# A two-layer graph network on one core: the first step's order, the last pair's tiles on three engines, and x in two transfers

## The reference

```python
# layer 0
h = jnp.maximum(_layernorm(x, axis=-1), 0.0)
query, keyt, value = h @ Wq.T + bq, h @ Wk.T + bk, h @ Wv.T + bv
weight = adj * jnp.exp(jnp.einsum('bqd,bkd->bqk', query, keyt))
weight = weight / jnp.sum(weight, axis=2, keepdims=True)
x = x + jnp.einsum('bqk,bkd->bqd', weight, value)
# layer 1
h = jnp.maximum(_layernorm(x, axis=-1), 0.0)
agg = jnp.einsum('bij,bjf->bif', adj, h) / jnp.maximum(deg, 1e-6)     # deg = sum of adj over its last axis
x = x + jax.nn.relu(jnp.concatenate([h, agg], axis=2) @ W.T)
```

## Time and profile before

| | |
|---|---|
| median of 3 runs | 1888.66 us (1887.45 to 1889.35) |
| the profiled execution's own time | 1885.8 us |
| its span | 1884.0 us |
| TensorE busy | 1866.5 us, 99% |
| VectorE, ScalarE, GpSimd busy | 1508.2, 894.1, 991.3 us |
| DMA | 370.70 MB, 197 GB/s over the span |

### The profile page before, as it was taken

The page is one execution under the profiler, slowest core; times in us unless marked ns, Lnnn a source line. Parts: engine busy times, 40 slices in busy tenths (PEclk is TensorE's granted clock), DMA queues, the critical chain, the costliest instruction groups (busy, mean ns, idle before and its releaser), DMA issues.

```text
span 1884.0 us, 29380 instructions
## 1 busy us (share of the span) xinstructions
PE 1866.5 (99%) x8900; PEld 1567.3 (83%) x8900; DVE 1508.2 (80%) x2677; ACT 894.1 (47%) x1661; POOL 991.3 (53%) x1032
## 2 busy tenths in 40 slices
PE   8999999999999999999999999999999999999998
PEld 5888888888888888888888888888888888888886
DVE  7788787887787888888877878887888778888776
ACT  4444544455444445444545444454445454444543
POOL 4655465464564554654644645545546546456452
PEclk9999999999999999999999999999999999999999
DMA  5766656656656656566666576565666665666632
GB/s 184 231 213 193 200 194 207 209 190 198 211 184 217 206 189 202 197 206 207 190 200 209 181 222 200 189 206 196 210 200 198 195 209 185 215 201 190 206 128 101
DMA packets 199809, 370.70 MB, mean 197 GB/s; under 512 B 18928, under 2 KB 116208, under 8 KB 199536
## 3 DMA queue, kind: packets, MB, share of 16 engines
q1 hardware_dynamic: 199792, 370.49, 61.4%
HBM read 266.60 MB, written 103.81 MB: 197 GB/s over the span
## 4 chain that ended last, share of the span: by engine, by line
PE 92%; DVE 3%; DMA 2%; POOL 1%; issue 1%; ACT 1%; SPq 0%; POOLq 0%; DVEq 0%
PE bank L532 30%; PE bank L533 30%; PE bank L534 30%; DMA turned_store<-blocks 1%; PE bank L550 1%; DVE h L1150 1%; POOL xb L417 0%; POOL hT_l L426 0%; DMA turned<-turned_store 0%; SPq L271 0%; DVE bank L1251 0%; DVE stats L1118 0%; POOL rs L405 0%; DVE x L1263 0%; DMA xb<-wk 0%
## 5 line engine op out<-in xcount | busy, mean ns | idle before, releaser
L421 POOL TENSOR_TENSOR hT_l<-turned,hT_h 128x512 fp32r<-128x512 f32 x122 | 155.3, 1298 | 348.4 <-ACT hT_h L852 348.3
L248 POOL TENSOR_TENSOR w_l<-w,w_h 128x512 fp32r<-128x512 f32 x64 | 83.5, 1304 | 377.4 <-ACT w_h L883 377.4
L1100 DVE STREAM_TRANSPOSE blocks<-h 128x512 f32<-128x512 f32 x252 | 163.7, 687 | 114.5 <-DMA turned_store<-blocks 113.8
L846 ACT ACTIVATE h<-x,rs 128x512 f32<-128x512 f32 x124 | 94.0, 806 | 236.9 <-POOL rs L411 236.9
L532 PE MATMUL bank<-hT_h,n_h 128*128 128x512 f32 x512 | 199.4, 389 | 1.2 <-DVE hT_l L1191 1.2
L532 PE MATMUL bank<-wv_h,hT_h 128*128 128x512 f32 x512 | 199.6, 390 | 0.0
L533 PE MATMUL bank<-wv_l,hT_h 128*128 128x512 f32 x512 | 199.6, 390 | 0.0
L533 PE MATMUL bank<-hT_l,n_h 128*128 128x512 f32 x512 | 199.2, 389 | 0.0
L534 PE MATMUL bank<-hT_h,n_l 128*128 128x512 f32 x512 | 199.2, 389 | 0.0
L534 PE MATMUL bank<-wv_h,hT_l 128*128 128x512 f32 x512 | 199.2, 389 | 0.0
L417 POOL TENSOR_TENSOR xb<-x_in,bv_b 128x512 f32<-128x512 f32 x128 | 167.6, 1322 | 8.9 <-issue 8.9
(11 more groups left out here) (154 smaller groups left out, 5307.9 us busy)
## 6 DMA issues: line engine op xcount, KB each, us to landing
turned_store<-blocks SPq DMA_DIRECT2D x126, 512.0 KB, 3.8
turned<-turned_store SPq DMA_DIRECT2D x504, 128.0 KB, 2.9
x_in<-x SPq DMA_DIRECT2D x32, 1024.0 KB, 5.8
n_h<-t_store SPq DMA_DIRECT2D x62, 512.0 KB, 4.5
n_l<-t_store SPq DMA_DIRECT2D x62, 512.0 KB, 5.7
out<-x SPq DMA_DIRECT2D x124, 256.0 KB, 2.1
n_h<-n_store SPq DMA_DIRECT2D x60, 512.0 KB, 4.6
n_l<-n_store SPq DMA_DIRECT2D x60, 512.0 KB, 5.7
```

What stands on the lines that cost most here:

```text
L248: engine.tensor_tensor(w_l[:, g], w[:, g], w_h[:, g].bitcast(F32), ALU.subtract).then_inc(w_split, 1)
L421: pool.tensor_tensor(by_blocks(hT_l, t), turned_tile(t), by_blocks(hT_h, t).bitcast(F32), ALU.subtract).then_inc(hT_split, 1)
L846: nc.scalar.activation(h[:, t, :], src[:, t, :], ACT.Relu, bias=rs[n][:, 1, t:t + 1], scale=rs[n][:, 0, t:t + 1]).then_inc(h_done[n], 1)
L1100: nc.vector.transpose(blocks[:, :, :, t % NT, :].rearrange("p j c b -> p c j b"), h[:, t, :].rearrange("p (c j b) -> p c j b", c=DT, b=Q)) ...
```

## The change

It has these parts.

- **SP.** x of pair 0 is loaded in two halves, one graph each, behind the first and the second rows of `wq` and `wk`. In `first_step` the two stores of `n` come first, T1's store moves behind both loads of turned blocks, next to T2's. The last pair's stores of tiles 0 and 1 wait for GpSimd's adds.
- **T2** is split into `kz_h` and `kz_l` (free by then) instead of `at_h` and `at_l`; its low part goes from GpSimd to VectorE.
- **GpSimd** in `first_step`: T1's low part moves behind the splitting of the weights, and the first two `low_hT` ahead of the fourth `mix`. In `final_step` it adds x for tiles 0 and 1.
- **ScalarE** in `first_step`: the exponentials come right behind `relu_norm`, ahead of `high_v` and T1; the copies of `hT` are put among those of `v`. In `final_step` it rectifies tiles 0 and 1 into `h`.
- **VectorE** in `first_step`: each `kz_l` follows its key bias, the statistics come behind them, `weigh(0, 0)` and `weigh(0, 1)` move to both sides of `turn_h(1, 1)`, the results and statistics of layer 0 come ahead of the last two key biases, and B11's low part moves to step 1, behind `kz_l`. In `final_step` it leaves L1255 out for tiles 0 and 1.

```diff
@@ SP, ahead of the steps
-                if o == 0:
-                    load_x(0)
+                if o < G:
+                    sp.dma_start(x_in[:, NT * o:NT * (o + 1), :], x_d[0][:, NT * o:NT * (o + 1), :]).then_inc(x_first[o], 16)
@@ SP, first_step
+                sp.wait_ge(n_split, DT)
+                sp.dma_start(n_d[0], n_h[:, :, :].bitcast(F32)).then_inc(n_stored, 16)
+                sp.dma_start(n_d[1], n_l[:, :, :].bitcast(F32)).then_inc(n_stored, 16)
                 store_blocks(0, 0, h_turned, NT, h_stored)
-                store_t(0, T1)
                 sp.wait_ge(h_stored[0], 16)
                 load_turned(0, 0, h_moved)
                 store_blocks(0, 1, h_turned, T, h_stored)
                 sp.wait_ge(h_stored[1], 16)
                 load_turned(0, 1, h_moved)
-                store_t(1, T2)
+                store_t(0)
+                store_t(1)
                 sp.wait_ge(w_split, G)
                 sp.dma_start(adj_in, adj_d[0]).then_inc(adj_loaded, 16)
-                sp.wait_ge(n_split, DT)
-                sp.dma_start(n_d[0], n_h[:, :, :].bitcast(F32)).then_inc(n_stored, 16)
-                sp.dma_start(n_d[1], n_l[:, :, :].bitcast(F32)).then_inc(n_stored, 16)
@@ SP, final_step
-                store_out(i - 1, x_in)
+                j = i - 1
+                for t in range(T):
+                    sp.wait_ge(*((last_x2, t + 1) if t < NT else (x2_done, T * j + t - NT + 1)))
+                    sp.dma_start(out_d[j, t], x_in[:, t, :]).then_inc(out_stored[t], 16)
@@ GpSimd, first_step
-                low_mix(T1)
                 pool.wait_ge(b_split, 1)
                 mix(wh_raw[1], wh_raw[1], wh_raw[0])
                 for g in range(G):
                     split_w(pool, 0, g)
-                low_mix(T2)
+                low_mix(T1)
+                for t in range(NT):
+                    low_hT(1, t)
                 pool.wait_ge(mixed, 3)
                 pool.wait_ge(b_split, 2)
                 mix(wz_raw[1], wz_raw[1], wh_raw[1])
-                for t in range(NT):
-                    low_hT(1, t)
                 low_at(0)
@@ GpSimd, final_step
+                for t in range(NT):
+                    pool.wait_ge(rectified, t + 1)
+                    pool.tensor_tensor(x_in[:, t, :], x_in[:, t, :], h[:, t, :], ALU.add).then_inc(last_x2, 1)
@@ ScalarE, first_step
-                high_v(0, 0)
-                act.wait_ge(mixed, 2)
-                high_mix(T1)
                 act.wait_ge(mix_split, T3)
                 for g in range(G):
                     exp(0, g)
+                high_v(0, 0)
                 for g in range(G):
                     high_w(0, g)
+                act.wait_ge(mixed, 2)
+                high_mix(T1)
+                high_v(0, 1)
                 act.wait_ge(mixed, 3)
-                act.wait_ge(t_stored, 32)
                 high_mix(T2)
-                high_v(0, 1)
                 high_v(0, 2)
+                high_hT(1, 0)
+                high_hT(1, 1)
                 high_v(0, 3)
-                act.wait_ge(v_psum, T)
-                for t in range(T):
-                    high_hT(1, t)
+                high_hT(1, 2)
+                high_hT(1, 3)
@@ ScalarE, final_step
+                for t in range(NT):
+                    act.wait_ge(y_done, T * j + t + 1)
+                    nc.scalar.activation(h[:, t, :], bank[AZ_BANK[t]][:, :], ACT.Relu).then_inc(rectified, 1)
@@ VectorE, first_step
                 for t in range(T):
                     key_bias_of(0, t, ahead=False)
-                low_kp(0, 0)
-                low_kp(0, 1)
+                    low_kp(0, t)
                 layer0_stats(1, 0)
-                low_kp(0, 2)
                 layer0_stats(1, 1)
-                low_kp(0, 3)
                 turn_h(1, 0)
                 low_b(B22)
+                weigh(0, 0)
+                turn_h(1, 1)
+                weigh(0, 1)
+                low_v(0, 0)
                 low_b(B21)
-                turn_h(1, 1)
-                low_v(0, 0)
-                for g in range(G):
-                    weigh(0, g)
                 low_v(0, 1)
+                key_bias_of(1, 0)
                 low_v(0, 2)
-                key_bias_of(1, 0)
+                key_bias_of(1, 1)
                 low_v(0, 3)
-                key_bias_of(1, 1)
-                sum_inverses(0, SUM_BANK, T + 1)
-                low_b(B11)
+                sum_inverses(0, SUM_BANK, y[:, :])
                 low_hT(1, 2)
                 low_hT(1, 3)
+                dve.wait_ge(mixed, 3)
+                dve.wait_ge(mix_split, T1)
+                layer0_result(0, 0, AV_BANK[0], x1)
+                layer1_stats(0, 0, x1)
+                layer0_result(0, 1, AV_BANK[1], x1)
+                low(kz_w[1], mix_raw[T2], kz_w[0], mix_high, T2, t2_split)
+                dve.wait_ge(mixed, 4)
+                dve.wait_ge(t2_split, 1)
+                layer0_result(0, 2, AV_BANK[2], x1)
+                layer1_stats(0, 1, x1)
+                moments(1, 0, 0)
+                layer0_result(0, 3, AV_BANK[3], x1)
+                layer1_stats(0, 2, x1)
+                layer1_stats(0, 3, x1)
+                moments(1, 0, 1)
                 key_bias_of(1, 2)
                 key_bias_of(1, 3)
-                dve.wait_ge(mixed, 4)
-                dve.wait_ge(mix_split, T2)
-                finish_layer0(0, AV_BANK, x1, None)
@@ VectorE, layer0
                 for dt in range(DT):
                     low_kp(i, dt)
+                if is_first(i):
+                    low_b(B11)
                 turn_g(j, 1)
@@ VectorE, final_step
                 sum_ha0(j, 0)
-                layer1_result(j, 0, AZ_BANK[0], x_in)
+                dve.wait_ge(part_split, 7 * j + S4)
+                layer1_y(j, 0, AZ_BANK[0])
                 sum_ha0(j, 1)
-                layer1_result(j, 1, AZ_BANK[1], x_in)
-                layer1_result(j, 2, AZ_BANK[2], x_in)
-                layer1_result(j, 3, AZ_BANK[3], x_in)
+                layer1_y(j, 1, AZ_BANK[1])
+                for t in range(NT, T):
+                    layer1_y(j, t, AZ_BANK[t])
+                    layer1_x(j, t, AZ_BANK[t], x_in)
```

70 lines of the change are left out of this document (44 added, 26 removed).

## The result

| | before | after |
|---|---|---|
| median of 20 runs each, side by side | 1887.6 us (1885.47 to 1892.87) | 1884.24 us |
| ratio | | 0.9982 (95%: 0.9976 to 0.9988) |
| profiled execution, its span | 1885.8, 1884.0 us | 1884.2, 1882.4 us |
| TensorE busy | 1866.5 us | 1866.1 us |

The kernel became 3.4 us faster (2.3 to 4.5), where the forecast was 0.2 us slower. The new median lies in the range and within 0.2% of no change, but the measurement tells it from none: the sign of the forecast was wrong. (One of the 20 runs of the kernel after took 2324.57 us; the others lie between 1882.0 and 1887.9, and it plays no part here.)

A forecast was written before the change was run, and what follows sets the result against it. TensorE, busy 1866.5 of 1884.0 us, was taken as the bound. Scores -0.45, clock +3.1, stall at 103.9 -0.7 and tail -1.75 gave +0.2 us, so a median of 1888.9 us, range 1883.2 to 1891.5.

The forecast's parts named there:

- the first term of the sum: Start of step 1's scores on TensorE: `kz_l` ready at 80.4 instead of 80.86, -0.45 us.
- x in two transfers: Opening loads: the second half of x lands later but nothing waits; 0, bounds -0.2 and +0.5 us.
- Key bias and `kz_l` in turn: First step: 2.93 us stall near 38 and its clock fall go; matmuls end at 43.8, 6.3 us earlier.
- Blocks behind the `n` stores: First step: `blocks` stored at 44.4, landing at 47.1; cost 0 if the queue drains, up to 3.9 us if not.
- the rival that made it slower: First step: undrained `n` stores delay `blocks` up to 3.9 us; +4.1 us in all, 1892.8; chance 0.10.
- VectorE's queue: Up to layer 0's results: 1.8 us TensorE stall, clock up, step 1's first `kp` at 61.6, 4.3 us earlier.
- The gate of step 1: Before step 1's scores: list takes 13.2 us from 61.5, then 5.6; gate at 80.4, stall about 5 us.
- The clock: Behind step 1's 5 us stall: granted clock falls again, +3.1 us, bounds 0 and 3.4.
- The stores of `n`: First step: moved early, at 31.6, behind the load of x; taken as costing 0.
- Later stalls: Behind step 1's scores: only the 0.7 us `hT_l` stall near 103.9 goes, -0.7; later small ones stay.
- The tail: Last step: two L1255 leave VectorE's chain, gaining 1.75 us, bounds 1.3 and 1.9.

The follow-up runs named there:

- e7: Kernel after, but ScalarE splits the next adjacency only once T2's low part is made, so GpSimd's `at_l` can't hold it; 1885.69 us.
- e12: e5 plus four more moves in the first step and step 1, meant to remove its remaining stalls; 1881.73 us, ratio 0.9969 to the kernel before.
- e3: Kernel after, but ScalarE's first two normalisations of step 1 wait for only two key biases; 1883.54 us, ratio 0.9979 to the kernel before.
- e4: Kernel after plus 15 useless matmuls ahead of step 1's scores, filling TensorE's stall; 1881.64 us, ratio 0.9973 to the kernel before.
- e9: Kernel after with the first x loaded in one transfer instead of two halves; 1883.76 us.
- e10: Kernel before with only the two stores of `n` moved to the front of SP's list; 1891.23 us.
- e8: Kernel after with the two stores of `n` back at their old place, behind adj; 1887.57 us.
- e11: Kernel before with only VectorE's first list reordered, each `kz_l` right behind its key bias, statistics following; 1885.66 us.
- e5: Kernel after with step 1's `kz_h` and `kz_l` of all tiles ahead of degrees and turning, plus e3's waits; 1880.21 us, ratio 0.9962 to the kernel before.
- e6: Kernel after with pair 1's last two key biases back ahead of layer 0's results; 1885.05 us, ratio 0.9982 to the kernel before.
- e1: Kernel after, unchanged, measured a second time; 1884.18 us, ratio 0.9984 to the kernel before.

## Why the prediction was wrong, point by point

**The step that failed is the first term of the sum**, "Scores of step 1: -0.45": `kz_l` was to be ready at 80.4 and was ready at 77.75, so the term measured -3.1. That is 2.65 of the 4.3 us between forecast and measured sum. The mechanism (a list of VectorE and ScalarE that ends later than TensorE arrives, and a clock that falls in the wait) was right; the length of the list was wrong. The later stalls were mis-sized by 1.2 us and the clock by 0.9, both the same way.

**x in two transfers: taken as 0; the first `kp` came 0.9 us earlier (0.8 on average).** The bounds (-0.2, +0.5) looked at x alone. What profits is the weights in the same queue: the second rows of `wk` land at 7.4 to 9.4 us with two halves, at least 0.5 us before TensorE takes them up, and at 10.2 to 11.5 with one transfer, at most 0.13 us before. The premise "TensorE is continuously busy from 4.00 to 38.2" was right for the trace of before, so no wait there accounts for the 0.9 us. It starts its first matmuls 0.85 us apart and later ones 0.43, and the closer spacing begins some 2 us later in before than in after (8 to 10 us of before, then of after; count of PE):

```profile
8.00:10.00 2.00, 2.00 (x4) 0.67 (x2) 1.01 (x2) 0.00 (x0) 0.00 (x0) 1.00 0.70 122
8.00:10.00 2.00, 2.00 (x6) 0.84 (x5) 1.12 (x6) 0.00 (x0) 0.83 (x2) 1.00 0.91 200
```

In before `wk` landed at 10.25 and was taken up at 10.38; in after TensorE was there at 9.49 and `wk` had landed at 8.47. So the gain needs both, the earlier `wk` and the earlier close spacing. The second isn't the change's doing: e7 and e12, with two halves, keep the wide spacing as long as before or longer and start their first `kp` at 24.41 and 24.58. That part of the 0.9 us is luck of the one profile. The earlier start arrives in full at the gate.

**Key bias and `kz_l` in turn: right.** The last `kz_l` was ready at 37.1 (forecast 38.0, less the earlier start), no stall, clock 1.00 in 41 to 47.3, as every kernel with that order has it.

**Blocks behind the `n` stores: right, and the rival that made it slower fell.** The first store of blocks was issued at 43.39 and had landed by 46.1, 2.7 us later, at 363 GB/s in 38 to 41. (At the 329 GB/s that the prediction names, its 3 MB end near 41, not 43; nothing hangs on it.)

**VectorE's queue: right in kind, 0.4 to 1.6 us too long.** Stall for `v_l` 1.38 us (1.8), `kp` of step 1 at 60.04 (61.6); 0.9 of the 1.6 us is the earlier start. The clock stayed up, as assumed.

**The gate of step 1: the wait was right, its end was forecast 2.65 us too late.** The relu of ScalarE started at 72.16 instead of 74.75, and from there to the first score it took 5.59 us, where 5.6 was forecast:

```profile
72.16 1.52 ACT L861 ACTIVATE h<-x,rs 128x512 f32<-128x512 f32 x2 [10.68 <-DVE key_bias L1173]
```

The 2.65 are 1.6 from the earlier beginning (59.9 for 61.5; 0.9 of it is the first `kp`) and 1.0 from the waits for GpSimd: between 59.9 and 72.1 the list took 12.2 us, not 13.2. T2 waited as I had put it (3.09 for 1.15 of its own; 1.9), but `mean_sum` waited 0.8 and 0.55 (forecast 1.2 and 0.75), and the last key biases nothing. These terms have no row in the trace of before, and the prediction said so; e7 shows that they can't be costed one by one. Here their sum was 1.0 us off. TensorE's own wait was 3.82 us instead of some 5. The 5.6 us were right for a reason that was half the truth: VectorE's degrees, turning and `kz_l` take as long as the relus of ScalarE that the prediction added up, as e3 shows.

**The clock: fell as said, price 3.1 forecast, 2.2 to 2.7 measured.** TensorE's lead over before was 3.1 us at the gate and 0.9 behind it; e4 gives 2.3 and 2.7. I had taken the price from the one row of before. At half rate TensorE made 5.15 us of work in after, 6.2 in before, 3.4 in e9; half of it is lost, so 1.7 to 3.1.

**The stores of `n`: costed at nothing, worth 3.3 us in the new order.** This didn't make the sum wrong, since the kernel has them early; but the prediction didn't see that the rest depends on it. I had asked what they delay (the blocks) and not what they release: step 1's loads over `n` wait for them, and behind these in SP's list stand x and the blocks. In before that wait is covered (e10); once the rest comes earlier it isn't (e8).

**Later stalls: wrong by 1.2 us.** I let the one at 103.88 go and kept the others, "because their chain starts from TensorE's own products". Both the one at 103.88 and the one at 162.31 went, and the lead rose from 0.9 to 2.8 us by step 3: 1.9 us, since the two stalls cost 0.96 and 0.91, more than the idle time by which I had priced the one. They hang on the loads of turned blocks: in e8 the one near 104 comes back when the blocks come later, in e12 both when TensorE comes earlier than the blocks do.

**The tail: 1.3 us at the end of the span, not 1.75.** VectorE's chain and the four stores at the end:

```profile
1877.11 2.73 SPq L394 DMA_DIRECT2D out<-x_in  x4
...
1877.22 0.69 DVE L1276 SCALAR_TENSOR_TENSOR x_in<-bank,x_in 128x512 f32<-128x512 f32 x1
1877.24 1.27 POOL L537 TENSOR_TENSOR x_in<-x_in,h 128x512 f32<-128x512 f32 x1 [0.16 <-ACT h L1109]
...
1878.61 0.69 DVE L1276 SCALAR_TENSOR_TENSOR x_in<-bank,x_in 128x512 f32<-128x512 f32 x1
```

From TensorE's end to the start of the last L1276 it is 1.14 us; it was 3.06. The chain is 1.9 us shorter, the upper bound, but the span's end only 1.3 nearer: from the end of the last L1276 it takes 3.1 us, where before took 2.5. The four stores are now issued within 2.8 us, the last three of them within 0.9, and the last two landed 2.3 and 2.5 us after their issue, where all four of before took 2.0. That they take longer because their transfers meet fits this, but wasn't tried. GpSimd's adds didn't hold VectorE: the L1276 of 1877.22 took 0.69 us beside one, as L1255 did without one in the earlier trace rows.

The Trainium skill, SBUF — State Buffer, section "Who interferes with whom", says that only a VectorE instruction with two SBUF inputs, or in a two-port mode, contends with GpSimd's reads. The trace agrees for L1276, which has one such input. The sums of `var_eps` (L1149) and L1164 have one too and were held in e7 and e6 (1.07 and 2.33 us); by the rule they would have to be in a two-port mode, which no run here shows.

**The sum again with what was measured:** gate -3.1 (0.9 of it the first `kp`), clock +2.2, the two `hT_l` stalls -1.9, tail -1.3: -4.1 us, against the measured -3.4 (-2.3 to -4.5). The forecast had -0.45, +3.1, -0.7 and -1.75. The gate is 2.65 of the difference, the later stalls 1.2, the clock 0.9, the tail -0.45.

**Where the expected gain of the change went.** e11 puts one list edit against the whole front: 157.37 us to step 3 against 157.97. The results ahead of the key bias, the split of T2, the move of B11 and of `n` bring step 1 forward by 4 us more than e11 does (36.6 against 40.7 us from the first `kp`), and all of it is given back at the gate in 73 to 84: 3.8 us idle and 2.2 us or more of clock. (These are single profiles, and the clock's share differs between them: 2.6 us of it lost in after, 3.1 in e11.) Both after and e11 win their time behind that point, by the two `hT_l` stalls. e5 goes 2.5 us beyond e11, so together with a step 1 list that fits they do hold a gain; what e5's list is worth without them wasn't run. What stays open is which of the edits inside the new first step are needed for that; they weren't undone singly, apart from the stores of `n` (needed) and the place of the last key biases (worth about 1.2 us, e6).

## What to carry to other kernels

When one engine is busy for 99% and a change brings it to a gate earlier, look first for what sets the gate and shorten that, since an engine that arrives early only waits, and a wait of 3 us is paid a second time in the clock. Ask of every moved DMA not only what it delays but which later load is waiting for it, and expect that its price is zero in one order and microseconds in another. Waits between VectorE and GpSimd belong to the stretch, not to an instruction: bound their sum (here it was off by 1 us), and don't count on removing one. Count a stall of TensorE from start to start of its matmuls, not by the idle time shown.

## What the runs showed of the hardware

- **The price of a stall in the clock varies.** Stalls of 3.82 us (after) and 3.79 us (e9), at the same place of the same work, were followed by half the clock during 5.15 and 3.4 us of TensorE's work. The stall for `kz_l` near 41 us was followed by 6.2 us of it in before (stall 2.93 us) and by at most 3.4 in e10 (2.87 us). One of 2.88 us (e11) halved it too; those of 1.38, 1.41, 1.91, 2.05 and 2.17 us (after, e3, e11, e12, e10) did not at once, though in e11 the clock was at 0.57 in 66 to 70, behind the one of 1.91 us.
- **Filling the wait of TensorE with 15 useless matmuls gained 2.6 us** (e4; front against e1), nearly as much as was left at step 3 of taking the wait away (e5, 3.0 us, of 5.8 won where the scores end).
- **A stall loses more than its idle time**: 0.26 to 0.27 us more at the matmuls of 128x512 that start 0.2275 us apart (0.96 for 0.69 us and 0.91 for 0.65 in before, 0.72 for 0.45 in e5, 2.32 for 2.05 in e12).
- **Tiny VectorE instructions wait as long as large ones**: 4 elements a partition took 0.55, 1.19 and 2.33 us in after, e7 and e6, by where GpSimd's instruction beside them ended. Sums over the free axis, statistics and transposes beside the same GpSimd instructions took their usual time (1.22 us for the 128x1024 sum in e6, 1.30 us for two transposes in after).
- **The 28 equal steps cost between 0.4 and 5.5 us more than 28 times one step**, in executions of the same or nearly the same code, mostly at waits for GpSimd's `hT_l`. What sets them off isn't known.
